# Relative attention in a two-layer decoder: adding the position bias and taking the row maximum in one VectorE operation per head

## The chip, the cores and the metric

The kernel runs on one core of a Trainium2 chip. The metric is the device time of one execution in microseconds (us); lower is better. TensorE (PE) does matrix products, VectorE (DVE) elementwise work and reductions, ScalarE (ACT) activations and copies, GpSimd (POOL) small powers and indirect DMAs, and SyncE (SP) issues most of the DMAs.

## The reference, cut to what matters

The reference is a two-layer decoder on an input of 32 batches x 112 tokens x 256 features. Each layer has an attention, a cross attention and a mixture of experts. The change touches only the last block's self attention, a relative attention with 16 heads of 16 features:

```
q, k, v = (x @ wq), (x @ wk), (x @ wv)            # each (Bs, Ss, H, HD), Ss = 112, H = 16
p = (pe @ wp).reshape(2 * Ss - 1, H, HD)
ac = jnp.einsum('bihd,bjhd->bhij', q, k)
bd_full = jnp.einsum('bihd,phd->bhip', q, p)
bd = bd_full[:, :, jnp.arange(Ss)[:, None], rel]
att = jax.nn.softmax((ac + bd) * scale, axis=-1)  # per head, over j
```

In the kernel's words, `ac` is "scores", `bd` is "bias", and `ac + bd` is "biased". The softmax needs the maximum of every row of `biased` for each head; all of it is in float32.

## The kernel before, in words

The decoder runs as a row of stages. The relative attention is the sixth, from about 2430 to 2830 us of the span, and the routed experts follow it.

The stage works batch by batch, in rounds that overlap. `RelativeAttention.__init__` lists the steps of a round with an age for each: in round e a step of age a works on batch e - a. Every engine runs its share of that list in the list's order, fully written out for the 32 batches. There is a set of steps for the attention itself and a set that sends the tokens to their experts (`Dispatch`): some of these run only in every fourth round, so that rounds come in four kinds. In this text they are called the route round (`gT0`, `gT1`, `route`, `choose1`), the rank round (`rank`, `choose2`), the match round (`choose3`) and the norm round (`gnorm`, `gscale`).

The steps that matter here, with the line of the instruction in the profile:

- Four banks of PSUM, `r_scores`, are used three times for a batch. `pos0` and `pos1` (PE, L2576) write the products of q with the positions into them, and `copy0` and `copy1` (ACT, L2612) take them out; a DMA writes them to memory and another reads them back shifted as `r_bias` (L2489, L2494). Two rounds later `scores` (PE, L2560) writes the products of q and k there.
- `add` (DVE, L2653) adds `r_bias` to `r_scores` for all 16 heads, 1792 elements in each of 112 partitions, and writes `r_biased` in SBUF. Its semaphore `added` releases `pos0` of a later batch, since the banks are free then: in round e, `add` is of batch e - 3 and `pos0` of batch e - 1.
- `top` (DVE, L2658) takes the 16 row maxima, `less` (DVE, L2661) subtracts them, and `exp` (ACT, L2618) makes the probabilities. `scale` (L819) stands between `add` and `top`, `again` (L2637) between `top` and `less`.
- `f0` to `f3` (PE, L1520) turn the probabilities, `heads` (PE, L1532) multiplies by v, `back`, `onT` and `project` (PE, L1563) finish a batch. DVE adds the projection to the stream at L2667.

PE's order in a round is `q`, `scores`, `f0`, `k`, `f1`, (`gT0`), `f2`, (`gT1`), `f3`, `onT`, (`route`), (`rank`), `pos0`, `heads`, `project`, `xT`, `pos1`, `back`, `v`. DVE's order is `add`, `scale`, `top`, `again`, `less`, `project`, (`choose1` to `choose3`), `gstats`, (`gnorm`), `tag`, `back`, (`gscale`), and then of the next round `stats`, `q`. Steps in brackets are those of every fourth round.

Each of `add`, `top` and `less` waits on a semaphore of the one before it.

Of the kernel before, what the change touches and what calls it, by code (L numbers as in the profile page):

```python
# [27 lines left out]
ALU = mybir.AluOpType  # L28
AX_X = mybir.AxisListType.X

P = 128
T = 112
D = 256
DC = D // P
H = 16
# [15 lines left out]
BIG = 1.5e38  # L51
# [98 lines left out]
def bc(ap, axis, n):  # L150

    v = ap.unsqueeze(axis)
    shape = list(v.shape)
    shape[axis] = n
    return v.to_broadcast(shape)


class Chain:
# [3 lines left out]
    def __init__(self, eng, sem, once=None):  # L162
        self.eng, self.sem, self.once = eng, sem, once
        self.base = self.n = self.k = 0
# [55 lines left out]
def at_least(eng, sem, n):  # L220

    if not isinstance(n, int) or n > 0:
        eng.wait_ge(sem, n)
# [122 lines left out]
def load_layer0(nc, G, stack, background):  # L346
# [24 lines left out]
    with ExitStack() as own:  # L371
# [58 lines left out]
        @block.vector  # L430
        def _(dve):
            for i, n in enumerate("qk"):
                for c in range(DC):
                    dve.wait_ge(folded, 2 * i + c + 1)
                    nc.vector.tensor_copy(W["w" + n][:, c, :], bank[2 * i + c][:, 0:D])
# [335 lines left out]
class Phase:  # L771
# [3 lines left out]
    scale = 1.0  # L775
# [375 lines left out]
class LatentAttention(Phase):  # L1151
# [4 lines left out]
    scale = XD ** -0.5 * XD ** -0.5  # L1156
# [433 lines left out]
class CausalAttention(Streamed):  # L1590

    tag = "a0"
    scale = HD ** -0.5
# [156 lines left out]
class RotaryAttention(Streamed):  # L1750
# [4 lines left out]
    scale = 24 ** -0.5  # L1755
# [160 lines left out]
class ContextAttention(Streamed):  # L1916

    tag = "x1"
    scale = HD ** -0.5
# [518 lines left out]
class RelativeAttention(Streamed):  # L2438
# [3 lines left out]
    scale = HD ** -0.5  # L2442

    def __init__(self, nc, G, W):
        super().__init__(nc, G, W)
        self.dispatch = G["dispatch"]
        self.plan = Timetable(4, [("stats", 0), ("q", 1), ("scores", 3), ("gs0", 12), ("add", 3), ("scale", 0), ("f0", 4),
                                  ("top", 3), ("k", 1), ("f1", 4), ("gT0", 6), ("f2", 4), ("gT1", 6), ("f3", 4),
                                  ("onT", 5), ("again", 0), ("less", 3), ("gs1", 12), ("route", 6), ("rank", 7),
                                  ("pos0", 1), ("copy0", 1), ("heads", 4), ("project", 5), ("choose1", 6), ("choose2", 7),  # L2450
                                  ("choose3", 8), ("gstats", 5), ("gnorm", 5), ("gpow", 5), ("tag", 11), ("xT", 0),
                                  ("pos1", 1), ("gs2", 12), ("back", 4), ("gscale", 5), ("copy1", 1), ("exp", 3),
                                  ("gcopy", 11), ("v", 1), ("gs3", 12)],
                                bankless=("stats", "scale", "again", "scores", "add", "top", "less", "exp", "pos0", "pos1", "copy0", "copy1",
                                          "gstats", "gnorm", "gpow", "gscale", "choose1", "choose2", "choose3", "tag", "gcopy",
                                          "gs0", "gs1", "gs2", "gs3"),
                                NB=self.NB, turns=3, behind=5, grouped=Dispatch.GROUPED, until=Dispatch.UNTIL)
# [170 lines left out]
    def dve(self, dve, name, b, par, c, body, chain):  # L2628
        nc, ring, X, S = self.nc, self.ring, self.X, self.G["S2"]
        if name == "stats":  # L2630
            self.norm_stats(self.norm, X[0:T, b, :], chain)
        elif name == "scale":
            chain.link(self.norm_scale(dve, self.norm, b, S[0:T, b, :], X[0:T, b, :]))
        elif name == "again":
            self.reuse(dve, "xT", b)
            dve.wait_ge(self.rstd2_ready, b + 1)
            nc.vector.tensor_scalar(self.xn[0:T, :], S[0:T, b, :], self.rstd2[0:T, :], None, ALU.mult).then_inc(self.xn_ready, 1)  # L2637
            if isinstance(b, int) and b == 0:
                for i in range(self.plan.turns):
                    nc.vector.memset(self.v[i][:], 1.0).then_inc(self.set_up, 1)  # L2640
        elif name == "q":

            bank = ring.take(dve, c, body)
            for p in range(2):
                ins = nc.vector.tensor_scalar(self.q[par][:, p, :, :].rearrange("p f t -> p (f t)"), bank[:, 0:DC * T],
                                              self.const("parity")[:, p:p + 1], None, ALU.mult)
            ring.freed(ins, c)
        elif name == "add":
            dve.wait_ge(self.scored, b + 1)
            for f in range(2):  # L2650
                dve.wait_ge(self.bias_loaded[f], b * 16 + 16)
            at_least(dve, self.exped, b)
            nc.vector.tensor_tensor(self.biased[0:T, :, :].rearrange("t (j f p) k -> t j f (p k)", j=4, f=2),  # L2653
                                    self.scores[0:T, :].rearrange("t (j c) -> t j c", c=512)[:, :, 0:4 * T].rearrange("t j (f k) -> t j f k", f=2),
                                    self.bias[par][0:T, :, :, :].rearrange("t f j k -> t j f k"), ALU.add).then_inc(self.added, 1)
        elif name == "top":
            dve.wait_ge(self.added, b + 1)
            nc.vector.tensor_reduce(self.tops[0:T, :], self.biased[0:T, :, :], AX_X, ALU.max).then_inc(self.topped, 1)  # L2658
        elif name == "less":
            dve.wait_ge(self.topped, b + 1)  # L2660
            nc.vector.tensor_tensor(self.biased[0:T, :, :], self.biased[0:T, :, :], bc(self.tops[0:T, :], 2, T),  # L2661
                                    ALU.subtract).then_inc(self.lessened, 1)
        elif name == "back":
            self.dve_back(dve, b, c, body, chain)
        elif name == "project":
            bank = ring.take(dve, c, body)
            ring.freed(nc.vector.tensor_tensor(S[0:T, b, :], bank[0:T, 0:D], S[0:T, b, :], ALU.add), c)  # L2667
        elif name in Dispatch.DVE:
            self.dispatch.dve(dve, name, b, c, chain)
# [712 lines left out]
```

## Time and profile before

| what | value |
|---|---|
| median of 3 runs | 3148.21 us (3142.97 to 3152.73) |
| the profiled execution | 3145.8 us, of which the span from the first to the last instruction is 3144.0 us |
| mean granted TensorE clock | 0.941 of full speed |
| PE busy | 2772.3 us (88%), 28144 matmuls |
| DVE busy | 2265.3 us (72%), 4822 instructions |
| ACT busy | 1664.6 us (53%), 3243 instructions |
| POOL busy | 960.8 us (31%), 1219 instructions |

The shares are means over stages that have different limits, so a change in one stage is read from that stage's own rows. In a timeline, a row's first number is when it starts and the second how long its instructions last together; an instruction's duration reaches on until its result is written, so the next one on the engine can start before it is over. The distance between two starts is what an instruction really costs its engine.

### The profile page before, as it was taken

To read this page: it belongs to the slowest core of one execution; us is meant where nothing else is said; L and a number is where in the kernel's file an instruction comes from. 1 tells how busy PE (TensorE), PEld (TensorE's weight loads), DVE (VectorE), ACT (ScalarE), POOL (GpSimd) and SP (SyncE) were. 2 spreads that over 40 slices of the span, in tenths; PEclk is the share of its full clock that TensorE was granted. 3 is DMA by queue.
4 is the path that set the end of the run, shared out by engine and by line. 5 is a ranking of instruction groups with operands and counts; after the bars stand their busy time and mean duration, and the time that the engine had idled before them with its cause. 6 is when DMAs were issued, how large, how long until landed. Compare 5 with 4: busy or idle time off the path is not lost. (4 is left out here: it accounts for less than half of the span.)

```text
span 3144.0 us, 75659 instructions
## 1 busy us (share of the span) xinstructions
PE 2772.3 (88%) x28144; PEld 2023.5 (64%) x28144; DVE 2265.3 (72%) x4822; ACT 1664.6 (53%) x3243; POOL 960.8 (31%) x1219
## 2 busy tenths in 40 slices
PE   7999899999999999676998799999997999983980
PEld 6887466666666666565886466666664777762970
DVE  5998567777777777567887577767763899984656
ACT  4777455555655555343554244444443788862540
POOL 0000344554554554460000100000000134545771
PEclk9999999999999999698999799999998999995995
DMA  7930354454455445262000333333330878856768
GB/s 179 295 100 0 110 158 132 138 166 152 135 160 162 137 149 155 76 200 87 0 0 1 65 73 73 73 68 73 73 62 23 235 229 235 248 172 201 223 193 254
DMA packets 364786, 413.70 MB, mean 132 GB/s; under 512 B 108016, under 2 KB 330512, under 8 KB 364368
## 3 DMA queue, kind: packets, MB, share of 16 engines
q1 hardware_dynamic: 218176, 220.63, 26.2%
q10 hardware_dynamic: 127216, 139.94, 15.1%
q0 software_dynamic: 19104, 49.22, 4.6%
q8 instruction: 188, 3.08, 0.4%
q14 instruction: 102, 0.84, 0.1%
HBM read 125.33 MB, written 252.45 MB: 120 GB/s over the span
## 5 line engine op out<-in xcount | busy, mean ns | idle before, releaser
L814 POOL TENSOR_TENSOR x_rstd<-x_var,g_minus_half 112x1 f32<-112x1 f32 x128 | 74.7, 584 | 707.3 <-DVE x_var L810 706.7
L2192 DVE TENSOR_REDUCE x_top<-x_scores 112x2 f32<-112x750 f32 x256 | 228.2, 932 | 81.1 <-PE x_scores L2036 80.6
L1369 ACT ACTIVATE x_probs<-x_held,x_minus_top 112x488 f32<-112x488 f32 x256 | 177.7, 697 | 173.4 <-DVE x_minus_top L1425 173.4
L1242 POOL TENSOR_TENSOR x_probs<-x_probs,x_inverse 112x488 f32<-112x488 f32 x256 | 250.6, 999 | 10.2
L1283 PE MATMUL x_ring<-w_xkv,x_kv 128*122 128x512 f32 x512 | 236.3, 594 | 0.0
L1276 PE MATMUL x_ring<-x_kv,w_xkv 128*128 128x488 f32 x512 | 232.6, 587 | 1.1 <-ACT x_kv L1345 1.1
L932 ACT ACTIVATE x_v<-x_ring 122x512 f32<-122x512 f32 (+1 forms) x224 | 113.1, 505 | 182.6 <-PE x_ring L1283 151.9
L2139 ACT ACTIVATE x_probsT<-x_scores 125x1792 f32<-125x1792 f32 x96 | 159.8, 1665 | 83.5 <-PE x_scores L2054 83.5
L1419 DVE SCALAR_TENSOR_TENSOR x_held<-x_scores,x_keep 112x976 f32<-112x976 f32 x128 | 150.3, 1174 | 74.0 <-PE x_scores L1296 51.6
L814 POOL TENSOR_TENSOR a_rstd<-a_var,g_minus_half 112x1 f32<-112x1 f32 x64 | 35.6, 556 | 535.9 <-DVE a_var L810 535.9
L1237 POOL TENSOR_TENSOR x_inverse<-x_sums,x_minus_one 112x2 f32<-112x2 f32 x128 | 89.7, 701 | 227.0 <-ACT x_probs L1369 227.0
L3100 POOL DMA_INDIRECT expert_replies<-m_rows,m_reply_of x143 | 138.4, 968 | 56.5 <-issue 31.1
L1424 DVE TENSOR_REDUCE x_top<-x_held 112x2 f32<-112x976 f32 x128 | 149.7, 1170 | 4.4
L1283 PEld LDWEIGHTS x_ring<-w_xkv,x_kv 128*122 128x122 f32 x512 | 91.7, 185 | 94.8 <-issue 93.2
L2036 PE MATMUL x_scores<-x_slots 32*112 32x375 f32 x1024 | 138.8, 529 | 13.7 <-DMA x_slots<-x_kq 7.6
L1304 PEld LDWEIGHTS x_ring<-g_constants,x_probs 112*122 112x122 f32 x1024 | 110.5, 139 | 55.0 <-issue 50.4
L1276 PEld LDWEIGHTS x_ring<-x_kv,w_xkv 128*128 128x128 f32 x512 | 90.6, 192 | 79.6 <-issue 74.6
L932 ACT ACTIVATE x_probsT<-x_ring 122x448 f32<-122x448 f32 x256 | 130.8, 540 | 1.8 <-PE x_ring L1304 1.6
L1321 PEld LDWEIGHTS x_ring<-x_probsT,x_v 122*64 122x64 f32 x2048 | 99.9, 138 | 47.1 <-issue 46.1
L1304 PE MATMUL x_ring<-g_constants,x_probs 112*122 112x112 f32 x1024 | 127.2, 261 | 2.5 <-POOL x_probs L1242 1.4
L2311 POOL DMA_INDIRECT expert_slots<-r_rows,d_slot_of x96 | 99.3, 1034 | 94.6 <-ACT r_by_position L2612 64.4
L1296 PE MATMUL x_scores<-x_k,x_q 64*112 64x488 f32 x512 | 122.4, 596 | 3.2 <-DVE x_held L1419 3.2
(471 smaller groups left out, 7350.8 us busy)
## 6 DMA issues: line engine op xcount, KB each, us to landing
expert_slots<-d_empty ACTq DMA_DIRECT2D x32, 3612.0 KB, 16.8
by_position<-r_by_position SPq DMA_DIRECT2D x64, 784.0 KB
first_slots<-d_empty SPq DMA_DIRECT2D x8, 3612.0 KB, 32.1
r_bias<-by_position SPq DMA_DIRECT2D x64, 392.0 KB
m_rows<-expert_slots SPq DMA_DIRECT2D x143, 129.0 KB
x_kq_swapped<-x_kq_raw ACTq DMA_DIRECT2D x64, 243.5 KB, 3.6
x_slots<-x_kq SPq DMA_DIRECT2D x512, 30.4 KB
m_rows<-expert_replies SPq DMA_DIRECT2D x32, 448.0 KB, 8.7
```

What stands on the lines that cost most here:

```text
L932: self.ring.freed(self.nc.scalar.activation(dst, src_of(bank), ACT.Copy), c)
L1242: self.nc.gpsimd.tensor_tensor(probs, probs, self.inverse[0:T, u:u + 1].to_broadcast([T, XK]), ALU.mult).then_inc(self.weighted, 1)
L1276: ins = nc.tensor.matmul(bank[:, 0:XK], W["xkv"][:, f, m * P:(m + 1) * P], self.kv[:, f, :], start=(f == 0), stop=(f == DC - 1))
L1283: ins = nc.tensor.matmul(bank[0:XCK, :], self.kv[:, f, i * XCK:(i + 1) * XCK], W["xkv"][:, f, 512:1024], start=(f == 0), stop=(f == DC - 1))
L1304: ins = nc.tensor.transpose(bank[0:XCK, i * T:(i + 1) * T], self.probs[u % 6][0:T, i * XCK:(i + 1) * XCK], self.const("ident", T)[:, 0:T])
L1369: nc.scalar.activation(self.probs[u % 6][0:T, :], self.held[m % 2][0:T, i, :], ACT.Exp, scale=self.scale, bias=self.minus_top[0:T, m % 2, ...
L1419: nc.vector.scalar_tensor_tensor(self.held[m % 2][0:T, :, :], self.scores[0:T, 1024 * (m % 2):1024 * (m % 2 + 1)].rearrange("t (i c) -> t ...
L1424: chain.link(nc.vector.tensor_reduce(self.top[0:T, m % 2, :], self.held[m % 2][0:T, :, :], AX_X, ALU.max))
L2036: ins = nc.tensor.matmul(self.scores[0:T, at:at + S2], slots[slot, g, S2:KQ], slots[slot, g, 0:S2], start=True, stop=True)
L2139: self.nc.scalar.activation(self.probsT[0:CK, i, :, :], self.scores[0:CK, at:at + 2048].rearrange("t (a c) -> t a c", c=512)[:, :, 0:HG * ...
L2192: nc.vector.tensor_reduce(self.top[0:T, g, 2 * half:2 * half + 2], self.scores[0:T, at:at + 1024].rearrange("t (a c) -> t a c", c=512)[:, ...
L3100: pool.indirect_dma_start(replies[:, :], bass.IndirectOffsetOnAxis(reply_of[:, j:j + 1], 0), rows[:, R + j % R, 0:D], None).then_inc(repli ...
```

## The change

`top` goes away as a step, and with it the semaphore that it gave. `add` becomes 16 instructions, one for each head, each of which adds the bias of its head (112 elements in 112 partitions), multiplies by 1.0, writes the sum to `r_biased` and gives the maximum of its row to `r_tops`. The semaphore `added` is given by the last of the 16, and `less` waits for it. Nothing is computed differently.

```
-                                  ("top", 3), ("k", 1), ("f1", 4), ("gT0", 6), ("f2", 4), ("gT1", 6), ("f3", 4),
+                                  ("k", 1), ("f1", 4), ("gT0", 6), ("f2", 4), ("gT1", 6), ("f3", 4),
...
-            nc.vector.tensor_tensor(self.biased[0:T, :, :].rearrange("t (j f p) k -> t j f (p k)", j=4, f=2),
-                                    self.scores[0:T, :].rearrange("t (j c) -> t j c", c=512)[:, :, 0:4 * T].rearrange("t j (f k) -> t j f k", f=2),
-                                    self.bias[par][0:T, :, :, :].rearrange("t f j k -> t j f k"), ALU.add).then_inc(self.added, 1)
-        elif name == "top":
+            for h in range(H):
+                j, f, p = h // 4, h // 2 % 2, h % 2
+                at = 512 * j + h % 4 * T
+                ins = nc.vector.tensor_tensor_reduce(self.biased[0:T, h, :], self.scores[0:T, at:at + T],
+                                                     self.bias[par][0:T, f, j, p * T:(p + 1) * T],
+                                                     1.0, -2 * BIG, ALU.add, ALU.max, self.tops[0:T, h:h + 1])
+            ins.then_inc(self.added, 1)
+        elif name == "less":
             dve.wait_ge(self.added, b + 1)
-            nc.vector.tensor_reduce(self.tops[0:T, :], self.biased[0:T, :, :], AX_X, ALU.max).then_inc(self.topped, 1)
-        elif name == "less":
-            dve.wait_ge(self.topped, b + 1)
```

## Rows read from the trace of the kernel before

**Rows 1.** Busy time by engine in a stretch of four rounds, one of each kind

```profile
core 0: us, PE busy (x) PEld busy (x) DVE busy (x) ACT busy (x) POOL busy (x), PEclk, DMA share, GB/s
2604.74:2652.96 48.22, 44.45 (x604) 37.10 (x604) 45.57 (x103) 41.02 (x60) 24.47 (x38) 1.00 0.82 239
```

**Rows 2.** Timeline of DVE, the match round: start us, us, what

```profile
2629.97 2.01 DVE L2653 TENSOR_TENSOR r_biased<-r_scores,r_bias 112x1792 f32<-112x1792 f32 x1
2631.90 0.40 DVE L819 TENSOR_SCALAR l_stream<-g_residual,r_mv,r_rstd 112x256 f32<-112x256 f32 x1
...
2634.28 0.34 DVE L2637 TENSOR_SCALAR r_xn<-l_stream,r_rstd 112x256 f32<-112x256 f32 x1
2634.54 2.02 DVE L2661 TENSOR_TENSOR r_biased<-r_biased,r_tops 112x1792 f32<-112x1792 f32 x1
2636.47 0.42 DVE L2667 TENSOR_TENSOR l_stream<-r_ring,l_stream 112x256 f32<-112x256 f32 x1
2636.81 0.68 DVE L2425 TENSOR_TENSOR r_match<-w_cb,r_gtops 112x512 f32<-112x512 f32 x1
...
2640.93 2.01 DVE L2653 TENSOR_TENSOR r_biased<-r_scores,r_bias 112x1792 f32<-112x1792 f32 x1
```

**Rows 3.** Timeline of PE, `pos0` of the match round and of the norm round

```profile
2632.24 1.02 PE L2576 MATMUL r_scores<-w_pT,r_q 32*112 32x224 f32 x16
...
2643.09 1.03 PE L2576 MATMUL r_scores<-w_pT,r_q 32*112 32x224 f32 x16 [0.46 <-DVE r_biased L2653]
```

**Rows 4.** Timeline of DVE, adds of early and late rounds

```profile
2455.79 2.02 DVE L2653 TENSOR_TENSOR r_biased<-r_scores,r_bias 112x1792 f32<-112x1792 f32 x1 [0.20 <-PE r_scores L2560]
...
2486.16 2.02 DVE L2653 TENSOR_TENSOR r_biased<-r_scores,r_bias 112x1792 f32<-112x1792 f32 x1 [0.28 <-PE r_scores L2560]
...
2508.47 2.02 DVE L2653 TENSOR_TENSOR r_biased<-r_scores,r_bias 112x1792 f32<-112x1792 f32 x1
...
2776.15 2.02 DVE L2653 TENSOR_TENSOR r_biased<-r_scores,r_bias 112x1792 f32<-112x1792 f32 x1
...
2796.25 2.02 DVE L2653 TENSOR_TENSOR r_biased<-r_scores,r_bias 112x1792 f32<-112x1792 f32 x1
```

**Rows 5.** Timeline of PE, `pos0` in the first round and in an early one

```profile
2445.93 1.02 PE L2576 MATMUL r_scores<-w_pT,r_q 32*112 32x224 f32 x16 [1.48 <-DVE r_biased L2653]
...
2478.58 1.02 PE L2576 MATMUL r_scores<-w_pT,r_q 32*112 32x224 f32 x16
```

**Rows 6.** Timeline of DVE, the route round and the bounds of rank and norm round

```profile
2604.74 2.01 DVE L2653 TENSOR_TENSOR r_biased<-r_scores,r_bias 112x1792 f32<-112x1792 f32 x1
...
2612.11 0.42 DVE L2667 TENSOR_TENSOR l_stream<-r_ring,l_stream 112x256 f32<-112x256 f32 x1 [0.79 <-PE r_ring L1563]
...
2619.00 2.01 DVE L2653 TENSOR_TENSOR r_biased<-r_scores,r_bias 112x1792 f32<-112x1792 f32 x1
...
2652.96 2.01 DVE L2653 TENSOR_TENSOR r_biased<-r_scores,r_bias 112x1792 f32<-112x1792 f32 x1
```

**Rows 7.** Timeline of PE, `pos0` of the route round

```profile
2609.10 1.02 PE L2576 MATMUL r_scores<-w_pT,r_q 32*112 32x224 f32 x16
```

**Rows 8.** A group of DVE by line and form, 2550 to 2750: count | busy us, mean ns | idle before

```profile
L2415 DVE TENSOR_TENSOR w_cb<-r_ring,w_wp 112x128 f32<-112x128 f32 x4 | 1.1, 278 | 0.0
```

**Rows 9.** Timeline of DVE, two linked small instructions of `choose1`

```profile
2614.34 0.09 DVE L2403 MATCH_VALUE_LOAD w_cb<-r_gtops,w_ao 112x8 f32 x1
2614.42 0.17 DVE L2403 MATCH_REPLACE8 w_cb<-r_gtops,w_ao 112x32 f32<-112x32 f32 x1
```

**Rows 10.** Timeline of ACT in an earlier stage: an accumulator read and the next instruction

```profile
1016.72 0.19 ACT L1369 ACTIVATION_READ_ACCUMULATOR x_probs<-x_held,x_minus_top 112x1 f32 x1
1016.81 0.69 ACT L1369 ACTIVATE x_probs<-x_held,x_minus_top 112x488 f32<-112x488 f32 x1
```

**Rows 11.** Busy time by engine in two stretches of 10 us; columns as in Rows 1

```profile
2400.00:2410.00 10.00, 5.70 (x154) 4.57 (x150) 1.00 (x4) 5.60 (x5) 0.00 (x0) 1.00 0.01 2
2440.00:2450.00 10.00, 6.39 (x86) 4.91 (x82) 7.02 (x7) 4.36 (x7) 1.67 (x5) 0.86 0.79 240
```

More of the change, by code:

```diff
@@ L2453, in __init__ @@
                                   ("gcopy", 11), ("v", 1), ("gs3", 12)],
-                                bankless=("stats", "scale", "again", "scores", "add", "top", "less", "exp", "pos0", "pos1", "copy0", "copy1",
+                                bankless=("stats", "scale", "again", "scores", "add", "less", "exp", "pos0", "pos1", "copy0", "copy1",
                                           "gstats", "gnorm", "gpow", "gscale", "choose1", "choose2", "choose3", "tag", "gcopy",
```

## The prediction

> **What bounds the kernel now.** I read the page's busy shares first, then the stage's own stretch, then the timelines of VectorE (DVE) and TensorE (PE) side by side. In four rounds of one kind each, 48.22 us, DVE is busy for 45.57 us, PE for 44.45 us, at a granted clock of 1.00 [rows 1]: two engines are nearly full, so the order in which they hand work to each other counts as much as their sums.
>
> In the match round DVE has no gap: add starts at 2629.97, the next at 2640.93, 10.96 us later [rows 2]. `pos0` of that round starts at 2632.24 without a wait, that of the next at 2643.09 after a wait of 0.46 for the add that began at 2640.93 [rows 2, 3]. So DVE bounds these rounds, and the end of `add` is already only just in time for PE. In the early rounds, without the dispatch's work, DVE waits 0.28 us for `scores` [rows 4]: there PE bounds.
>
> There is a loop through the four PSUM banks: `add` ends, `pos0` may write, then `heads`, `project`, `xT`, `pos1`, `back`, `v`, `q`, `scores`, and the next `add`. From `pos0` at 2478.58 to the add at 2486.16 it takes 7.58 us where PE never waits [rows 4, 5]. From the end of add's share of DVE (start to start 1.93, 2629.97 to 2631.90) to `pos0` it is 2643.09 - 2640.93 - 1.93 = 0.23 us [rows 2, 3]. With A for what `add` occupies DVE, a round can't be shorter than A + 0.23 + 7.58. Today that is 9.74 us, hidden under 10.96.
>
> **The change part by part.** *Removed.* From add to less DVE takes 2634.54 - 2629.97 = 4.57 us; 1.93 are add, 0.26 `again` (2634.28 to 2634.54), and I put 0.35 for `scale`, which with the wait behind it takes 0.44 (2631.90 to `top`) at most [rows 2]. What is left, about 2.0 us, is `top` and its waits. `less` stays as it is.
>
> *Added.* 16 operations of 112 elements with a maximum. No row shows this operation, so I bound it. The part that adds: a PSUM add of 1792 elements costs 1.93 us start to start, one of 256 elements 0.34 (2636.47 to 2636.81) [rows 2], so an element costs 1.035 ns and 112 elements cost 0.34 - 144 x 0.001035 = 0.19 us. The maximum must then leave the engine's accumulator. ScalarE does that with an instruction of its own, ACTIVATION_READ_ACCUMULATOR, which takes 0.09 us start to start [rows 10]; DVE's smallest linked instruction, a load of 8 values, takes 0.08 [rows 9]. I take 0.08, so T = 0.27 us per head and A = 16 x 0.27 = 4.32 us. The ends: 0.19 with no read at all (A = 3.04), and 0.45 if neither instruction overlaps the next, from their durations: 278 ns for a PSUM add of 128 elements, 0.26 for 112 [rows 8], and 0.19 for the read [rows 10] (A = 7.2). I stay near the lower end because DVE's neighbouring rows all overlap.
>
> The accumulator read is also what the Trainium skill has (VectorE: DVE Perf Modes, "Two Vector instructions with no wait between them"): an operation that writes out its accumulator is two instructions. Only ScalarE's rows show it here [rows 10].
>
> The same page (section "The TRN2 errata") speaks against this change: the fixed cost is paid per instruction, 120 cycles with a PSUM source and 58 with SBUF, so small tiles pay it again and again. As an estimate from that page the pair costs (120 + 112 + 58 + 1) / 0.96 = 303 ns, A = 4.85 and the sum below would be about 52 us. The trace doesn't agree in size: its 256-element PSUM add costs 0.34, the page's formula gives 0.39 [rows 2].
>
> *On DVE alone* the change is small: `less` would come A + 0.35 + 0.26 = 4.93 us after add's start instead of 4.57, +0.36 a round.
>
> *Moved, and this is the main term:* `added` used to be given when the banks had been read once, in 1.93 us. Now it comes with the last head, after 4.32, since the maximum is taken while they are read. `top` read SBUF and held no bank. Behind `pos0` on PE's queue stand `heads`, `project`, `xT`, `pos1` and all the rest. A round's lower bound becomes 4.32 + 0.23 + 7.58 = 12.13 us. DVE also waits for PE in `project`: that came 6.50 us after add (2629.97 to 2636.47); in the route round, where it waited for PE, it came 2612.11 - 2609.10 = 3.01 after `pos0` [rows 2, 6, 7]; it will come 4.32 + 0.23 + 3.01 = 7.56 after add, +1.06, and what stands behind it on DVE moves with it.
>
> *Round by round,* 31 distances between adds:
> - First: PE waited 1.48 us for `add` [rows 5], so the whole growth shows: 4.32 - 1.93 = +2.39.
> - Next five, 2455.79 to 2508.47, 52.68 us [rows 4]. Four become 12.13. The fifth is a norm round like 2640.93 to 2652.96, 12.03 us [rows 2, 6], and becomes 13.09. 4 x 12.13 + 13.09 = 61.61: +8.9.
> - Five groups of four. Route: `pos0` came 4.36 after add (2604.74 to 2609.10), behind PE's own work, now 4.55: +0.19 [rows 6, 7]. Rank: 10.97 (2619.00 to 2629.97) to 12.13, +1.16. Match: 10.96 to 12.13, +1.17. Norm: +1.06. Sum 3.58, times five: +17.9.
> - One more route and rank round: +1.35. Two late rounds, 2776.15 to 2796.25, 20.10 us [rows 4], become 24.26: +4.2.
> - The last distance has slack; the last `less` is late by about +0.4.
>
> Together 35 us. The following stage starts when this one ends, so all of it shows: 3145.8 + 35.1 = 3180.9 against the profiled execution, which is 2.4 below the median of the runs. From the median: 3148.2 + 35.1 = 3183.
>
> How it moves with T: 0.01 us of T is 0.16 us of A, about 4 us of the total below T = 0.26 and 5 us above, where the route rounds lengthen too.
>
> **The rivals.**
> 1. *Not slower: one instruction per head, no read.* Place: the 16 operations. At T = 0.19, A = 3.04 and the bound is 10.85, 0.1 under what the DVE-bound rounds have. Early and late rounds still lose, the others win little: +2 us, 3150. It decides from T = 0.21 on, where the loss reaches 9.4 us (0.3%). For a real gain an operation would have to cost less than about 0.18, hardly its elements' own 0.12 and DVE's 0.06 that the small rows leave [rows 9]. Against it: ScalarE's separate read.
> 2. *DVE's sum alone decides.* If PE could make up the delay of `pos0` elsewhere, a round would grow by 0.36: 31 x 0.36 = +11, 3159. Against it: the early rounds, where PE's path of 7.58 stands without a gap.
> 3. *Small instructions don't overlap.* If the read or the next head waits until the result is written: 0.26 + 0.08 = 0.34, A = 5.44, +70, 3218; with both durations in full, 0.45, +125, 3273. For it: the read depends on the instruction ahead of it. Against it: the linked pair [rows 9], where a load of 8 values holds the next back by 0.08.
> 4. *The clock.* PE would stand still for over 1 us in each round. In one stretch with PE busy for 6.39 of 10 us the granted clock was 0.86, between its levels of 1.2 and 2.4 GHz; in another with 5.70 it was 1.00, the level of 2.4 GHz [rows 11]. At 0.86, 7.58 would become 8.81: 31 x 1.23 = +38 on top, 3221. PE would still be busy for about 44.4 of 51.8 us, so it isn't likely.
>
> **How the numbers follow.** The forecast, 3183, with T from 0.235 to 0.30 (3168 to 3198): 0.60. Rival 1: 0.08. Rival 2: 0.10. Rival 3: 0.14, of which 0.06 near its upper end. Rival 4: 0.08. The range 3156 to 3235 leaves out rival 1, the lower part of rival 2 and the upper end of rival 3, about 0.18. A measurement of this kernel can tell about 0.3% from no change. Slower by more than that: the forecast, rivals 3 and 4 and most of rival 2, 0.88. Within it: most of rival 1 and the rest of rival 2, 0.10. Faster: 0.02.
>
> **What would show it.** Right: 16 adding rows and 16 reads per batch, 0.27 apart in pairs; `pos0` waiting for `r_biased` in every round but the route round, by 1.5 us and more; `scores` awaited by `add` in the rank and match rounds; adds 12.1 us apart there; DVE idle ahead of L2667 by about 0.5. Wrong: rounds of 10.9 us, a DVE without gaps, or a single row per head. The prediction fails most easily on T, which no row shows, and on what I take to be fixed: PE's 7.58.

## The result, and the profile after

| | before | after |
|---|---|---|
| median of 6 runs each, us | 3145.34 (3142.97 to 3152.73) | 3158.78 (3155.56 to 3164.43) |
| the profiled execution, us | 3145.8 | 3164.43, span 3162.6 |
| mean granted TensorE clock | 0.941 | 0.939 |
| DVE busy, us | 2265.3, 4822 instructions | 2248.2, 5782 instructions |

The ratio is 1.0039 [1.0027, 1.0051]: the change makes the kernel slower, by 13.4 us. The forecast was slower by 35. The sign and the range held, the size did not. The page of the kernel after:

```profile
span 3162.6 us, 76590 instructions
PE 2777.8 (88%) x28144; PEld 2027.1 (64%) x28144; DVE 2248.2 (71%) x5782; ACT 1663.3 (53%) x3243; POOL 958.4 (30%) x1219
```

VectorE is busy for 17 us less and the kernel still takes longer. The timeline of DVE in a rank round of the kernel after (start, us; its `less` is now L2662, its projection L2668):

```profile
2620.22 0.26 DVE L2656 CUSTOM_DVE_ANT_0 r_biased<-r_scores,r_bias 112x112 f32<-112x112 f32 x1
2620.41 0.08 DVE L2656 DVE_READ_ACCUMULATOR2_ANT r_tops<- 112x1 f32 x1
2620.41 0.27 DVE L2656 CUSTOM_DVE_ANT_0 r_biased<-r_scores,r_bias 112x112 f32<-112x112 f32 x1
...
2623.33 0.08 DVE L2656 DVE_READ_ACCUMULATOR2_ANT r_tops<- 112x1 f32 x1
2623.33 0.41 DVE L819 TENSOR_SCALAR l_stream<-g_residual,r_mv,r_rstd 112x256 f32<-112x256 f32 x1
2623.77 0.35 DVE L2637 TENSOR_SCALAR r_xn<-l_stream,r_rstd 112x256 f32<-112x256 f32 x1
2624.04 2.02 DVE L2662 TENSOR_TENSOR r_biased<-r_biased,r_tops 112x1792 f32<-112x1792 f32 x1
```

Every head is a pair, as forecast, but the read starts at the same instant as the next head's addition. 2623.33 - 2620.22 = 3.11 us for 16 heads is 0.1945 us each: the 0.08 us of the read are not added to it (what the maximum and its read cost together, 0.013 us, is measured below). So A, the time for which `add` holds the banks, is 3.11 us, not 4.32; it was 1.93 in [rows 2]. `less` comes 2624.04 - 2620.22 = 3.82 us after add's start, where it came 4.57 after it.

The waits from 2460 to 2820, of the kernel after and then of the one before (us in total, times, longest):

```profile
DVE l_stream L2668 <- PE r_ring L1563: 29.1, 28, 3.8
PE r_scores L2576 <- DVE r_tops L2656: 19.9, 23, 1.6
```

```profile
DVE l_stream L2667 <- PE r_ring L1563: 8.7, 7, 2.4
PE r_scores L2576 <- DVE r_biased L2653: 4.8, 11, 0.5
```

VectorE's saving turned into waiting for `project`, because PE itself now waits for VectorE ahead of `pos0` (L2576) in 23 rounds, up to 1.6 us, where it had waited in 11, up to 0.5 us. The timeline of PE of the kernel after has these `pos0` in the route, rank, match and norm round of a group that runs at full clock:

```profile
2726.05 1.02 PE L2576 MATMUL r_scores<-w_pT,r_q 32*112 32x224 f32 x16
...
2739.29 1.03 PE L2576 MATMUL r_scores<-w_pT,r_q 32*112 32x224 f32 x16 [1.59 <-DVE r_tops L2656]
...
2750.25 1.03 PE L2576 MATMUL r_scores<-w_pT,r_q 32*112 32x224 f32 x16 [0.57 <-DVE r_tops L2656]
...
2761.21 1.02 PE L2576 MATMUL r_scores<-w_pT,r_q 32*112 32x224 f32 x16 [0.57 <-DVE r_tops L2656]
```

The distances from rank to match and from match to norm are 10.96 us each. The bank loop gives A + 0.23 + 7.58 = 10.92 for A = 3.11: it bounds them. And in three of the six route rounds PE ran at half clock for a while. The timeline of PE of the kernel after:

```profile
2623.50 0.35 PE L2334 MATMUL r_ring<-d_route,w_aq 128*112 128x32 f32 x2 [0.67 <-ACT w_akc L2352]
...
2625.16 1.51 PE L2576 MATMUL r_scores<-w_pT,r_q 32*112 32x224 f32 x16
2626.61 1.72 PE L1532 MATMUL r_ring<-r_probsT,r_v 112*32 112x112 f32 x32
2628.26 1.45 PE L1563 MATMUL r_ring<-w_ro,r_normedT 128*112 128x256 f32 x4
```

and its windows just before and in that place (columns as in Rows 1; the number ahead of DMA share is the granted clock):

```profile
2620.20:2625.00 4.80, 4.13 (x43) 3.95 (x42) 4.76 (x36) 3.81 (x9) 3.33 (x7) 1.00 0.92 243
2625.00:2630.00 5.00, 5.00 (x61) 3.62 (x64) 1.31 (x2) 2.54 (x4) 0.76 (x1) 0.66 0.42 125
```

`heads` (L1532) takes 0.97 in an undisturbed round and 1.72 here. From this `pos0` to the step behind `project` it takes 4.39 us (2625.16 to 2629.55), against 2.81 in the undisturbed route round (2726.05 to 2728.86): 1.6 us late, at a mean clock between the levels of 1.2 and 2.4 GHz. The `pos0` in which the clock falls waited for nothing. PE's last wait ahead of it was 0.67 us for ScalarE, in the route step (L2334), and the kernel before has that wait too (0.62 us).

To separate the stage from the rest of the program I take its length from the first `less` to the last, a distance that the change doesn't move by itself: 365.43 us before, 375.87 after, +10.4. This is the sum by kinds of round, in distances between `less`:

| | before | after | growth | forecast |
|---|---|---|---|---|
| first six | 64.71 | 67.89 | +3.2 | +11.3 |
| five groups of four | 240.87 | 246.97, of it 3.2 half clock | +6.1 | +17.9 |
| last route round and what follows | 59.85 | 61.01 | +1.2 | +5.9 |

In the last line both kernels had a half-clock route round (15.83 before, 16.55 after; at full clock 14.26 and 14.91), and the kernel before a second half-clock stretch in its last distance. The clock is also low for some us at the first `less`, in both kernels; where the text says that no round lost the clock, it means the rounds after that.

### The profile page after: what moved, and what is told of

Read it like the earlier page. It is cut to its first block and busy times, and to the rows that moved or that the text cites. A ratio compares the mean times of both kernels' runs of the same rounds, so it can differ in the third digit from the quotient of the medians.

```text
span 3162.6 us, 76590 instructions
## 1 busy us (share of the span) xinstructions
PE 2777.8 (88%) x28144; PEld 2027.1 (64%) x28144; DVE 2248.2 (71%) x5782; ACT 1663.3 (53%) x3243; POOL 958.4 (30%) x1219
## 5 line engine op out<-in xcount | busy, mean ns | idle before, releaser
L2612 ACT ACTIVATE r_by_position<-r_scores 112x1792 f32<-112x1792 f32 x64 | 106.6, 1665 | 49.8 <-PE r_scores L2576 49.7
```

## The experiments

My theory: the bank loop, A + 0.23 + 7.58, with A from the 16 heads, sets the early, match and late rounds, and half clock, brought on by PE's new waits, adds the rest. Its rivals were that VectorE's own sum decides, that PE could be relieved by another order, and that the half clock is chance.

**Is it the moment of release?** The kernel before, with its one `add` and its `top`, but `pos0` waiting for `top`. Nothing is computed otherwise.

```
-                at_least(pe, self.added, b - 1)
+                at_least(pe, self.topped, b - 1)
```

> The kernel before, with one wait changed: pos0 may write the score banks only when the row maximum (top) of the earlier batch is done, not when its add is done. DVE's work is untouched. Theory 1 (a round is bound by the loop through the banks: time from add's start to the release, + 0.23, + 7.58 us): the release comes 1.93 + 0.44 + 1.94 = 4.31 us after add's start instead of 1.93, the rank and match rounds go from 10.96 to about 12.1, the early ones from 10.3 to 12.1, in all +33 us or more (about 3178). Theory 2 (the sum of DVE's work alone sets the rounds): no change, within 3 us.

Measured: 3221.06 against 3151.76 us (4 and 11 runs), ratio 1.0214 [1.0196, 1.0232], +69 us; the stage is 434.8 us long. The timeline of DVE, two `less` of an early round at full clock, then that of PE in a later round:

```profile
2489.77 2.02 DVE L2661 TENSOR_TENSOR r_biased<-r_biased,r_tops 112x1792 f32<-112x1792 f32 x1
2501.89 2.02 DVE L2661 TENSOR_TENSOR r_biased<-r_biased,r_tops 112x1792 f32<-112x1792 f32 x1
```

```profile
2743.52 1.02 PE L2576 MATMUL r_scores<-w_pT,r_q 32*112 32x224 f32 x16 [1.73 <-DVE r_tops L2658]
2744.48 1.59 PE L1532 MATMUL r_ring<-r_probsT,r_v 112*32 112x112 f32 x32
2746.00 2.05 PE L1563 MATMUL r_ring<-w_ro,r_normedT 128*112 128x256 f32 x4
```

and a window of 60 us:

```profile
2650.00:2710.00 60.00, 51.97 (x628) 42.62 (x621) 47.83 (x107) 42.80 (x64) 24.87 (x41) 0.89 0.72 200
```

The release comes at A = 4.31 here, and the undisturbed round is 12.12 us: 4.31 + 0.23 + 7.58. So the loop was read rightly, and the 33 us that it gives would have been the whole cost at full clock. The other 36 are what is left over, and they fit the clock: it fell about twenty times between the first and the last `less`, with PE at half speed behind or at the end of waits of 1.73 us and more, and an early round so hit is 1.6 us longer (13.70 against 12.12). This is my rival 4, which I had called unlikely, in a kernel whose A is what I had forecast for the change.

**What does splitting cost, and what the maximum?** The kernel before with 16 plain additions; `top` stays.

```
-            nc.vector.tensor_tensor(self.biased[0:T, :, :].rearrange("t (j f p) k -> t j f (p k)", j=4, f=2),
...
+            for h in range(H):
...
+                ins = nc.vector.tensor_tensor(self.biased[0:T, h, :], self.scores[0:T, at:at + T],
+                                              self.bias[par][0:T, f, j, p * T:(p + 1) * T], ALU.add)
+            ins.then_inc(self.added, 1)
```

> The kernel before, with the add of all heads split into 16 plain adds of 112 elements, without a maximum; top stays. If the accumulator read costs the engine nothing, the adds stand 0.195 us apart, as the operations with the maximum do in the changed kernel; if it costs something, they stand closer, down to 0.17. DVE's work grows by 16 x 0.195 - 1.93 = 1.2 us a round in some 25 rounds that DVE bounds, and the bank loop becomes 10.9 us, which lengthens five early rounds by 0.6: +32 us (about 3177). If only the release of the banks counted: +5 to +13 us.

Measured: 3177.86 against 3151.76 us (4 and 11 runs), ratio 1.0079 [1.0059, 1.0099], +26 us. The timeline of DVE: the additions of a match round, and two early `less`:

```profile
2701.16 2.98 DVE L2656 TENSOR_TENSOR r_biased<-r_scores,r_bias 112x112 f32<-112x112 f32 x16
2704.07 0.40 DVE L819 TENSOR_SCALAR l_stream<-g_residual,r_mv,r_rstd 112x256 f32<-112x256 f32 x1
```

```profile
2502.05 2.02 DVE L2664 TENSOR_TENSOR r_biased<-r_biased,r_tops 112x1792 f32<-112x1792 f32 x1
2512.76 2.02 DVE L2664 TENSOR_TENSOR r_biased<-r_biased,r_tops 112x1792 f32<-112x1792 f32 x1
```

16 plain additions take 2704.07 - 2701.16 = 2.91 us, 0.182 each; with the maximum they take 0.1945. So the maximum and its read cost 0.013 us a head, and the splitting 2.91 - 1.93 = 0.98 us a batch. Of the 1.18 us by which the change lengthens A, most is thus the splitting and not the maximum. The early round is 10.71 us, and the loop gives 2.91 + 7.81 = 10.72. In the match round (11.90) VectorE's sum bounds instead: 10.96 + 0.98 = 11.94. What the change saves by dropping `top` is thus real: the splitting alone, with `top` kept, costs 26 us against the change's 13, and the stage is 385.8 us long against 375.9.

**Does VectorE's sum bound the kernel after?** An unread maximum of two constants, 448 elements, behind each `less`.

```
+            at_least(dve, self.topped, b)
+            nc.vector.tensor_tensor(self.filler[0:T, :], self.const("keep0", T), self.const("keep0", T),
+                                    ALU.max).then_inc(self.topped, 1)
```

> The changed kernel, with one more DVE operation behind less in every round: a maximum of a table with itself into a tile that nobody reads, 448 elements, about 0.53 us start to start. Theory 1 (PE and the banks set the rounds, DVE waits for PE ahead of L2668, 29 us in all in the changed kernel's trace): the wait takes it up, the time is that of the changed kernel within 4 us. Theory 2 (DVE's sum of work sets them): 32 x 0.53 = +17 us against the changed kernel.

Measured: 3158.48 against 3152.31 us (12 and 27 runs), ratio 1.0020 [1.0005, 1.0035]. The timeline of DVE:

```profile
2658.55 2.02 DVE L2662 TENSOR_TENSOR r_biased<-r_biased,r_tops 112x1792 f32<-112x1792 f32 x1
2660.49 0.62 DVE L2665 TENSOR_TENSOR r_filler<-g_constants 112x448 f32<-112x448 f32 x1
2661.09 0.42 DVE L2671 TENSOR_TENSOR l_stream<-r_ring,l_stream 112x256 f32<-112x256 f32 x1
```

0.60 us more per batch fill the gap ahead of the projection (no wait is left in the last row), the match and rank rounds stay at 10.96 and 10.9, but for one rank round of 12.46 with half clock, and the stage is 376.7 us long. The kernel after, run again beside it (next experiment), took 3157.56 us with a stage of 375.8. So 0.9 us came of the 17 that a bound by VectorE's sum would have given. VectorE's sum doesn't decide in the kernel after.

**Is the half clock chance?** The kernel after again, unchanged.

> The changed kernel once more, beside the three others on one chip. The same ratio, 1.004, and a stage about 10 us longer than before's; how many stretches at the lower clock fall into its route rounds is seen in its profile: 2 more than before's in the first profile, each with some 1.6 us. If they are chance, their number changes here and the rank and match rounds at the full clock stay at 10.9 to 11.0 us.

Measured: 3157.56 against 3152.31 us (12 and 27 runs), ratio 1.0014 [0.9999, 1.0029]. The stage is 375.78 us long, and the same three route rounds carry the half clock (16.85, 16.48 and 16.53 us; 16.86, 16.51 and 16.55 in the first trace). The stage repeats to 0.1 us, so in this kernel the half clock isn't chance. (With the unread work of the last experiment the same three rounds had it, and one more.) The total doesn't repeat as well: +5 here, with an interval that includes no change, and +13 at first.

**Can PE be kept at full clock?** The kernel after with unread transposes on PE, 6 ahead of the route step's products and 10 ahead of the rank step's. The first fill the wait of 0.67 us for ScalarE, the others part of the rank round's wait of 1.59 us.

```
+            for i in range(6):
+                nc.tensor.transpose(bank[0:T, i % 4 * T:(i % 4 + 1) * T], phase.const("ident", T)[:, 0:T], phase.const("ident", T)[:, 0:T])
             phase.ready(pe, "gT0", b, c)
...
         elif name == "rank":
+            for i in range(10):
+                nc.tensor.transpose(bank[0:T, i % 4 * T:(i % 4 + 1) * T], phase.const("ident", T)[:, 0:T], phase.const("ident", T)[:, 0:T])
             pe.wait_ge(self.chosen, g + 1)
```

> The changed kernel, with products that nobody reads where PE waits in the route and rank rounds: 6 transposes of a constant ahead of route's wait and 10 ahead of rank's, about 0.1 us each, in the bank that the step has claimed. They take the place of waits. Theory 1: the stretches at the lower clock in the third and fourth route round (3.5 us of the stage's 10.4) come from PE's idle time; they vanish, and route rounds of 16.5 to 16.9 us become 14.9, -3.5 us in the stage. Rival: they have another cause and stay where they are.

Measured: 3155.16 against 3148.89 us (12 and 23 runs), ratio 1.0018 [1.0007, 1.0029]. The timeline of PE at the transposes, and its waits from 2460 to 2800, of this kernel and then of the kernel after:

```profile
2613.19 0.79 PE L2331 MATMUL r_ring<-g_constants 112*112 112x112 f32 x6
...
2615.55 1.03 PE L2580 MATMUL r_scores<-w_pT,r_q 32*112 32x224 f32 x16
2616.51 0.97 PE L1532 MATMUL r_ring<-r_probsT,r_v 112*32 112x112 f32 x32
```

```profile
PE r_scores L2580 <- DVE r_tops L2660: 14.1, 23, 0.9
```

```profile
PE r_scores L2576 <- DVE r_tops L2656: 18.7, 21, 1.6
```

`heads` stays at 0.97, the route rounds are 14.91 (one 15.29), all without half clock, and the stage is 371.03 us long: 4.8 less than the kernel after. (One stretch lies in the last distance, which is 12.44 us with it as it was without.) So it is idle time of PE that costs the clock in the route rounds, as far as one trace shows it. Which of the two gaps matters isn't separated here; the last experiment below, with the first six transposes alone, speaks for the route step's. In the total the gain can't be told from the run-to-run spread (1.0018 here, 1.0014 for the kernel after on another chip).

**The kernel before once more,** unchanged, a single run on the chip of the last experiment.

> The kernel before once more, for its profile alone. Theory 1: first to last less takes 365.4 us within 0.5, with a single route round (the last) lengthened by the lower clock, as in the first profile; what the runs differ by lies outside this stage.

Measured: 3160.16 us, a single run, and a stage of 362.57 us, not the 365.4 of the first trace. The difference is that this time no round lost the clock, so in the kernel before the stretches do come and go: the last route round is 14.26 (15.83 then), and the distance to the last `less` is shorter:

```profile
2809.19 2.03 DVE L2661 TENSOR_TENSOR r_biased<-r_biased,r_tops 112x1792 f32<-112x1792 f32 x1
2821.53 2.02 DVE L2661 TENSOR_TENSOR r_biased<-r_biased,r_tops 112x1792 f32<-112x1792 f32 x1
```

The last distance is 12.34, against 13.41 in the first trace. So without half clock the stage is 362.6 us before and 371.0 with the change: +8.5 us of dependence, and about 5 of clock. Outside the stage this run was 2795.8 us long and the first trace of the same kernel 2778.6, while the kernel after had 2786.7 and 2782.6: most of the spread between totals is made there. In the window from 300 to 340 us, in an earlier stage, PE's granted clock was 0.66 in this run (row below) and 0.83 in the first trace:

```profile
300.00:340.00 40.00, 26.42 (x189) 18.26 (x188) 19.91 (x51) 13.63 (x26) 4.93 (x14) 0.66 0.06 17
```

**Can PE do something else while it waits?** Two orders were tried, each on both kernels. First `heads` ahead of `pos0`:

```
-                                  ("pos0", 1), ("copy0", 1), ("heads", 4), ("project", 5), ("choose1", 6), ("choose2", 7),
+                                  ("heads", 4), ("pos0", 1), ("copy0", 1), ("project", 5), ("choose1", 6), ("choose2", 7),
```

On the kernel after, and then on the kernel before:

> The changed kernel, with heads (0.90 us on PE) ahead of pos0 on PE and ahead of copy0 on ACT, so that PE has work while it would wait for the banks, and the loop through the banks is shorter by 0.90. Theory 1: the loop falls from 3.11 + 0.23 + 7.58 = 10.92 to about 10.0 us, DVE's own work of about 10.2 us or PE's of 10.3 sets the rank and match rounds, and the change's saving on DVE shows: about -12 us against before (3133), -25 against the changed kernel. Theory 2 (the loss comes from DVE's sum or from something outside this stage): as the changed kernel, +13 us against before.

> The kernel before with the same new place for heads. DVE bounds its rank and match rounds with 10.96 us of gapless work, and the bank loop (9.74 us) was hidden: theory 1 expects no change, within 3 us of before. If the new order brings something by itself, it shows here and has to be taken off the run of the changed kernel with the same order.

Measured: 3166.59 against 3151.76 us, ratio 1.0049 [1.0036, 1.0063], and 3170.87, ratio 1.0066 [1.0051, 1.0081]. Both expectations missed. The first one's second theory gave about this total (+13), but its reason, VectorE's sum, was excluded above; the rows show another one. The timeline of PE, of the changed kernel with `heads` first:

```profile
2643.35 1.03 PE L2576 MATMUL r_scores<-w_pT,r_q 32*112 32x224 f32 x16 [0.51 <-DVE r_tops L2656]
2646.15 1.03 PE L2576 MATMUL r_scores<-w_pT,r_q 32*112 32x224 f32 x16 [0.53 <-ACT r_by_position L2612]
...
2654.03 0.97 PE L1532 MATMUL r_ring<-r_probsT,r_v 112*32 112x112 f32 x32 [0.59 <-ACT r_probsT L932]
```

`heads` had covered `copy0`: with less between `pos0` and `pos1`, PE waits for ScalarE's copy instead (0.53), and `heads` itself comes too soon for its input (0.59). Early rounds are 11.6 us in both kernels, at full clock; two route rounds of the first and four of the second have half clock besides. Second, `v` ahead of `pos0`, with a fourth buffer for it (the edit below, and `range(4)` and `b % 4` where the buffers of `v` are made, filled and read):

```
-                                  ("pos0", 1), ("copy0", 1), ("heads", 4), ("project", 5), ("choose1", 6), ("choose2", 7),
+                                  ("v", 1), ("pos0", 1), ("copy0", 1), ("heads", 4), ("project", 5), ("choose1", 6), ("choose2", 7),
...
-                                  ("gcopy", 11), ("v", 1), ("gs3", 12)],
+                                  ("gcopy", 11), ("gs3", 12)],
```

> The changed kernel, with v (0.86 us on PE, needed by nobody in this round) moved from between pos1 and scores to the place ahead of pos0, where PE waits 0.57 us and more for the banks, and a fourth buffer for v. Nothing of what covers copy0 is moved. Theory 1: PE's path from pos0 to the next scores gets shorter, but only by about 0.46, since scores then waits for copy1 (pos1 to the end of copy1 is 2.8 us, and 3.28 - 0.86 = 2.42 us of PE's work lie between). The loop falls from 10.92 to about 10.5, rank and match rounds with it, and the time is 8 to 14 us under before (about 3140). Theory 2 (heads-first was slower because any change of PE's order costs): slower than the changed kernel, +15 us or more against before.

> The kernel before with the same new place for v and the fourth buffer. Its rank and match rounds are bound by DVE (10.96 us without a gap), so theory 1 expects no change, within 4 us. If it gains as much as the changed kernel does with this order, the gain is the order's and not the fused operation's.

Measured: 3168.61 against 3152.31 us, ratio 1.0055 [1.0033, 1.0076], and 3170.16, ratio 1.0055 [1.0037, 1.0073]. Again both missed, with the same ratio and the same early round, 11.19 us, though the two kernels hold the banks for 3.11 and 1.93 us. The timeline of PE, the kernel with `v` early:

```profile
2477.61 0.57 PE L1520 MATMUL r_ring<-g_constants,r_probs 112*112 112x112 f32 x4 [0.58 <-ACT r_probs L2618]
...
2480.25 1.03 PE L925 MATMUL r_ring<-w_rv,r_xT 128*112 128x256 f32 x4
2481.21 1.02 PE L2576 MATMUL r_scores<-w_pT,r_q 32*112 32x224 f32 x16
```

There is another loop, one that I hadn't drawn. These are its rows in an early round of the kernel before, between the `pos0` of 2478.58 and the next at 2488.90: `pos1` (PE), `copy1` and `exp` (ACT), `f0` (PE).

```profile
2481.68 1.03 PE L2576 MATMUL r_scores<-w_pT,r_q 32*112 32x224 f32 x16
2482.77 1.66 ACT L2612 ACTIVATE r_by_position<-r_scores 112x1792 f32<-112x1792 f32 x1 [0.20 <-PE r_scores L2576]
2484.34 1.69 ACT L2618 ACTIVATE r_probs<-r_biased 112x1792 f32<-112x1792 f32 x1
2486.17 0.57 PE L1520 MATMUL r_ring<-g_constants,r_probs 112*112 112x112 f32 x4 [0.16 <-ACT r_probs L2618]
```

PE's work from `pos0` to `pos1` takes 3.10 us, `copy1` starts 1.09 later, `exp` 1.57 after that, `f0` 1.83 after that, and from `f0` to the next `pos0` PE needs 2.73: together 10.32, which is why these rounds are 10.32 and not the 9.74 of the bank loop. `v` ahead of `pos0` lies in the last part (3.60 from 2477.61 to 2481.21 above) and adds its own 0.87: 10.32 + 0.87 = 11.19, whatever A is. So neither of the two orders could fill PE's wait for nothing; that no other can isn't shown. The second theory for the changed kernel, that any change of PE's order costs, had the number right (+15 or more), but it names no cause, and the rows do.

**A version that takes half of each.** The kernel before, with heads 8 to 15 added by one plain instruction of 896 elements, whose maxima a plain reduction takes after the banks are given back, and heads 0 to 7 by the new operation.

```
-            nc.vector.tensor_tensor(self.biased[0:T, :, :].rearrange("t (j f p) k -> t j f (p k)", j=4, f=2),
...
+            nc.vector.tensor_tensor(self.biased[0:T, 8:16, :].rearrange("t (j f p) k -> t j f (p k)", j=2, f=2),
...
+                                    self.bias[par][0:T, :, 2:4, :].rearrange("t f j k -> t j f k"), ALU.add).then_inc(self.halved, 1)
+            for h in range(H // 2):
...
+                ins = nc.vector.tensor_tensor_reduce(self.biased[0:T, h, :], self.scores[0:T, at:at + T],
+                                                     self.bias[par][0:T, f, j, p * T:(p + 1) * T],
+                                                     1.0, -2 * BIG, ALU.add, ALU.max, self.tops[0:T, h:h + 1])
+            ins.then_inc(self.added, 1)
         elif name == "top":
+            dve.wait_ge(self.halved, b + 1)
+            nc.vector.tensor_reduce(self.tops[0:T, 8:16], self.biased[0:T, 8:16, :], AX_X, ALU.max).then_inc(self.topped, 1)
+        elif name == "less":
             dve.wait_ge(self.added, b + 1)
-            nc.vector.tensor_reduce(self.tops[0:T, :], self.biased[0:T, :, :], AX_X, ALU.max).then_inc(self.topped, 1)
...
```

PE, not shown here, waits for `halved` as well as for `added` before it writes the banks.

> A mix: two banks (8 heads) by one plain add and later one plain maximum of 896 elements, the other two by 8 fused operations. Theory 1: the release comes at A = 1.00 + 8 x 0.195 = 2.56 us, the bank loop is 2.56 + 0.23 + 7.58 = 10.4; DVE's work falls by 0.3 a round to 10.65, which bounds the rank and match rounds. So these rounds go from 10.96 to about 10.65, and the stage from first to last less from 365.4 to about 360 us (without stretches at the lower clock): about 5 us under before, some 15 under the changed kernel. If any fused operation costs by itself, it is slower than before by half of what the changed kernel is.

Measured: 3145.73 against 3148.89 us (12 and 23 runs), ratio 0.9989 [0.9975, 1.0004]: not told from no change. The timeline of DVE, one such `add`, and two early `less`:

```profile
2668.57 1.08 DVE L2655 TENSOR_TENSOR r_biased<-r_scores,r_bias 112x896 f32<-112x896 f32 x1
2669.56 0.26 DVE L2661 CUSTOM_DVE_ANT_0 r_biased<-r_scores,r_bias 112x112 f32<-112x112 f32 x1
...
2671.11 0.41 DVE L819 TENSOR_SCALAR l_stream<-g_residual,r_mv,r_rstd 112x256 f32<-112x256 f32 x1
```

```profile
2492.47 2.02 DVE L2671 TENSOR_TENSOR r_biased<-r_biased,r_tops 112x1792 f32<-112x1792 f32 x1
2502.84 2.02 DVE L2671 TENSOR_TENSOR r_biased<-r_biased,r_tops 112x1792 f32<-112x1792 f32 x1
```

A is 2671.11 - 2668.57 = 2.54 us, the bank loop 10.35, just above the other loop's 10.32: early rounds are 10.36 or 10.37. The match round, DVE's own, is 10.66 (10.65 expected). One route round lost the clock (15.96 against 14.39), and so did the last distance (14.04), so the stage is 363.26 us long and not the 360 expected. So I gave this version the 6 transposes of the route step too:

> The mix of half plain and half fused heads, with the 6 unread transposes ahead of route's wait. The mix's profile had one route round of 15.96 us, where the clock fell, beside others of 14.39. Theory 1: with PE busy there the route rounds are all 14.4, the stage from first to last less is about 361 us, and the time 4 to 7 us under before. If the clock falls for another reason, a route round of 16 stays.

Measured: 3142.08 against 3151.15 us (12 and 17 runs), ratio 0.9973 [0.9961, 0.9986]: faster than the kernel before, and so than the one after. The stage is 360.07 us long, 2.5 less than the undisturbed stage before, and the match round 10.67. None of its route rounds has half clock any more, though a stretch remains in the last distance (12.47, against 12.34). The total's 9 us are more than the stage's 2.5 to 5.4; the rest I can't place, and the same transposes in the kernel before, without the mix, weren't run.

## Why the prediction was wrong in size

**The failed step is T.** The prediction put 0.19 us for adding a head, which was right (0.182 as a plain addition, 0.1945 with the maximum), and 0.08 on top for the accumulator's read, taken from two other kinds of instruction [rows 9, 10]. The read has its own row, of 0.08 us, but runs beside the next head. T is 0.1945 and A 3.11. Rival 1 gave +2 us at 0.19, and by the forecast's slope, 4 us for 0.01 of T, 0.1945 gives about +4, where 0.27 gave +35. The text had bounded T from 0.19 to 0.45 and chosen 0.27: the truth lay at the lower bound, and rival 1, "no read", had 0.08. As to form it was wrong (there is a read), as to price it was right.

That an operation with an accumulator is two instructions is what the Trainium skill says (VectorE: DVE Perf Modes, "Two Vector instructions with no wait between them"), and the rows agree. The same page of the Trainium skill, in the section "The TRN2 errata", had given the estimate of 303 ns for the pair. The rows show 194.5 from start to start, so that its fixed costs are not paid in full here by neighbours that wait for nothing.

**The bank loop was right.** Three values of A give its round to 0.04 us: 2.91 gives 10.72 (measured 10.71), 3.11 gives 10.92 (10.96), 4.31 gives 12.12 (12.12). 7.58 stayed fixed at full clock. The early rounds of before were bounded by the loop through `copy1` and `exp`, not by PE's work alone, but that changed no term: the bank loop exceeds it from A = 2.51 on.

**The route rounds were mis-sized the other way.** I wrote +0.19 for them, since `pos0` of the route round comes behind PE's own work. But the `pos0` after it, of the rank round, waits for an `add` that follows the projection, and that follows `pos0` by 3.01 us: 3.01 + 6.89 + A + 0.23, with 6.89 from 2612.11 to 2619.00 [rows 6]. It was 12.06 and is 2739.29 - 2726.05 = 13.24: the whole growth of A, 1.18. Ahead of it the route round itself got shorter, from 14.22 (2594.88 to 2609.10 in the timeline of PE before) to 13.49, since it had waited 0.57 us for q and no longer does. Net +0.45 per group of four (48.21 to 48.65), where my way of summing gives -0.2 at A = 3.11: five times 0.65, and once more for the sixth route round, is +3.9. With the +4 from T this is an estimate of 7.9, and 8.5 is measured between the undisturbed stages. (It is rough: the five groups grew by 0.35 to 0.86, not by 0.45 each.)

**The clock** was a rival of 0.08 with 38 us. At the real A it costs 4.8 in the stage, three stretches of 1.6 us; at the A that I had forecast it would have cost 36 (the first experiment). The argument against it, that PE would still be busy for 44.4 of 51.8 us, was no argument: in the window of that experiment PE was busy for 51.97 of 60, nearly the same share, and the granted clock was 0.89. So the forecast of 3183 was probably too low for its own assumption: going by that experiment, T = 0.27 would have meant about 3148 + 69 = 3217, an estimate, since the change itself was never run with such a T.

**That the range held is luck.** With the measured T, and all else as forecast, the sum gives 3148 + 4 = 3152, below the range's 3156. The route rounds (+3.9) and the clock (+4.8), which the sum had left out, come on top: from the 3145.34 of the result's own table, 4 + 3.9 + 4.8 give 3158.0, and 3158.78 was measured, 3 us inside the range. With the +5 us of the repeat it would have been outside. T too high and two terms too low went against each other.

**The signs named in advance.** Right: 16 pairs of rows in a batch; `pos0` waiting for the adding operations except in the route round; DVE idle ahead of the projection by 0.5 (0.51 in most rounds). Wrong: pairs 0.27 apart, waits of 1.5 us (0.57 in most rounds, 1.59 only in the rank round), rounds of 12.1 us. In between: no wait of `add` for `scores` is listed in the rank and match rounds, but `add` starts 0.87 us after `q` there (2756.99 to 2757.86) where it took 0.71 before (2640.22 to 2640.93), a delay of 0.16. "Rounds of 10.9 us" was listed as what would show the forecast wrong, and it did. Rival 2, DVE's sum alone, is excluded by the 0.60 us of unread work that changed no round at full clock; rival 3 by the distance of 0.1945.

**What stays open.** The two comparisons of the kernel after give +13.4 and +5 us, with intervals that barely overlap (1.0027 to 1.0051 and 0.9999 to 1.0029), while its stage repeats to 0.1 us. The stages before and behind it vary by more than that between two runs of one kernel, so the total can't be pinned closer than 5 to 13 us by these runs. Nor do the rows tell why the half clock hits the third, fourth and last route round and not the others, whose waits are nearly the same, or whether the transposes of the route step alone would have kept it away in the kernel after.

## What to carry to other kernels

Fusing two passes over a buffer saves the second pass but can lengthen the hold on what the first one read. Here the PSUM banks were held for 1.18 us more, 0.98 of them because one instruction had to become 16. Before costing the saving, write down every loop through that buffer, with the hold as one term, and compare each loop's sum with the round. A mix can be the better trade: the mixed version kept 0.3 us a round of the saving and half of the early release (A = 2.54, between 1.93 and 3.11). Where a change makes PE wait in every round, the granted clock is a cost of its own, to be read from a run and not argued away from PE's busy share.

## What the runs showed of the hardware

- VectorE's accumulator read (0.08 us, its own row) starts together with the next instruction and hardly delays it: 0.1945 us a head with the maximum and its read, 0.182 without, for 112 elements from PSUM. One add of 1792 such elements takes 1.93 us, 16 adds of 112 take 2.91.
- With waits of 1.73 us and more in PE, round after round, the granted clock fell about twenty times in the stage (0.89 over 60 us, `heads` 1.59 to 1.72 us instead of 0.97), and an early round so hit was 1.6 us longer. In the kernel after, with waits of 0.57 to 1.59 us, it fell in the same three route rounds in both traces. Unread transposes in PE's gaps took these stretches away (375.8 to 371.0 us).
- The granted clock of an early stretch that no kernel here touches (300 to 340 us) was 0.83 in one run of the kernel before and 0.66 in another; where such totals differ by 0.3%, a stage's own length says more than they do.
